# Feed-forward half of a two-layer gated block: values in chunk pairs, rounding on VectorE, four result rows

## The reference

```python
def act_quant(x):
    scale = 127.0 / jnp.clip(jnp.max(jnp.abs(x), axis=-1, keepdims=True), 1e-05)
    return jnp.clip(jnp.round(x * scale), -128, 127) / scale
...
h = bit_linear(x, w1)                              # 512 -> 2048
h = depthwise_conv1d(h.transpose(0, 2, 1), conv_w, conv_b)   # 3 taps along the tokens
h = h.transpose(0, 2, 1)
h = jax.nn.silu(h)
return bit_linear(h, w2)                           # 2048 -> 512
```

## Time and profile before

| | us |
|---|---|
| median of three executions | 2200.01 |
| lowest and highest | 2198.89, 2200.37 |
| profiled execution: time | 2204.66 |
| profiled execution: span of the core | 2202.7 |
| mean granted TensorE clock | 0.938 of full |
| busy in the span: DVE | 1763.1 |
| PE | 1642.2 |
| ACT | 1581.0 |
| POOL | 578.2 |

### The profile page before, as it was taken

The page is one execution under the profiler, slowest core; times in us unless marked ns, Lnnn a source line. Parts: engine busy times, 40 slices in busy tenths (PEclk is TensorE's granted clock), DMA queues, the critical chain, the costliest instruction groups (busy, mean ns, idle before and its releaser), DMA issues.

```text
span 2202.7 us, 24527 instructions
## 1 busy us (share of the span) xinstructions
PE 1642.2 (75%) x9542; PEld 735.0 (33%) x9542; DVE 1763.1 (80%) x2630; ACT 1581.0 (72%) x1157; POOL 578.2 (26%) x438
## 2 busy tenths in 40 slices
PE   7868766886588578659886888899887566667664
...
GB/s 179 1 20 68 20 1 20 67 20 1 1 6 20 44 1 6 6 96 327 199 257 142 68 93 96 96 99 84 80 65 58 24 48 48 48 48 48 39 34 34
DMA packets 104549, 143.65 MB, mean 65 GB/s; under 512 B 8046, under 2 KB 61422, under 8 KB 104050
## 3 DMA queue, kind: packets, MB, share of 16 engines
...
## 4 chain that ended last, share of the span: by engine, by line
ACT 40%; PE 35%; DVE 14%; DMA 5%; issue 3%; POOL 2%; POOLq 0%; SPq 0%; DVEq 0%; ACTq 0%
ACT unit L514 35%; PE psum L1579 5%; PE psum L1613 5%; PE psum L1659 4%; PE psum L1565 4%; DVE hmax_parts L1394 3%; PE psum L1009 3%; PE psum L1015 2%; DMA out_rows<-x3in 2%; DVE unit L423 2%; PE psum L1589 2%; DVE psum L1386 2%; PE psum L1606 1%; DMA xblk<-xnT_scratch 1%; PE psum L1598 1%
## 5 line engine op out<-in xcount | busy, mean ns | idle before, releaser
L514 ACT ACTIVATE unit<-unit 128x4096 f32<-128x4096 f32 x244 | 857.4, 3610 | 0.5 <-DVE unit L423 0.3
L423 DVE TENSOR_SCALAR unit<-feat_proj,text_proj 128x1024 f32<-128x1024 f32 x976 | 667.4, 746 | 66.6 <-PE psum L639 64.7
L639 PE MATMUL psum<-unit,w_pad 128*32 128x512 f32 x3904 | 471.8, 601 | 236.6 <-ACT unit L514 236.6
L639 PEld LDWEIGHTS psum<-unit,w_pad 128*32 128x32 f32 x3904 | 102.2, 109 | 556.9 <-ACT unit L514 399.6
L1659 PE MATMUL psum<-w_q,hidden_q 128*128 128x512 fp8e4 x512 | 144.7, 447 | 77.0 <-ACT hidden_q L1548 39.1
L1637 PE MATMUL psum<-xq_block,w_q 128*128 128x512 bf16 x512 | 140.4, 413 | 45.8 <-ACT hidden L1530 45.4
L1737 POOL TENSOR_TENSOR hidden<-hidden,srow 128x2048 f32<-128x2048 f32 x32 | 144.7, 4524 | 90.4 <-ACT srow L1534 90.4
L680 POOL TENSOR_SCALAR red<-red 128x8 f32<-128x8 f32 x4 | 2.0, 508 | 531.4 <-DVE red L321 531.4
L1518 ACT ACTIVATE psum<-h,conv_b_sb,conv_w_sb 128x512 f32<-128x512 f32 x128 | 98.3, 776 | 47.6 <-DVE h L1380 43.9
L1579 PE MATMUL psum<-xnT_c,wq_sb 128*128 128x256 f32 x512 | 121.7, 392 | 11.0 <-ACT xnT_c L1470 11.0
L547 PE MATMUL psum<-xnT,W_sb 128*128 128x512 f32 x256 | 125.2, 617 | 2.1 <-ACT xnT L465 2.1
...
## 6 DMA issues: line engine op xcount, KB each, us to landing
...
x<-in_x SPq DMA_DIRECT2D x32, 256.0 KB, 2.9
x_scratch<-x SPq DMA_DIRECT2D x32, 256.0 KB, 2.1
x3in<-x_scratch SPq DMA_DIRECT2D x31, 256.0 KB, 2.7
```

The costliest lines, as they stand in the source:

```text
L423: ins = ve.tensor_scalar(units[:, n % 3, k, :], FP[:, bi % 2, k, :], TP[:, k, n:n + 1], None, ALU.add)
L514: ac.activation(units[:, n % 3], units[:, n % 3], ACT.Tanh).then_inc(unit_tanh, 1)
L639: mm = te.matmul(psum[k * TG:(k + 1) * TG, 3 + 2 * grp + half, :], w_pad[:, k, TG - 1 - tt:2 * TG - 1 - tt], units[:, n % 3, k, half * BAN ...
```

## The change

- `H2` and `h2q` are laid out as [8 pairs, tokens, 2]: the values of chunks 2g and 2g + 1 for a token stand side by side. SILU writes every second element; HMAX reduces over pair and chunk-in-pair; HS repeats each value of `srow` twice; W2 loads its weights with a step of two elements.
- HRA and HRB on ACT become HROUND on DVE: one tensor_scalar that adds and subtracts MAGIC and writes bf16. HS of a tile after the first waits until the tile before it is rounded.
- x3in has four buffers, and load_rows(t) waits for the store of tile t - 4.
- `last_tokens` is cut into four parts, issued in the last block ahead of W2 and of OUT of tile i; its SiLU follows SROW. The reload of the four rows is issued among the last tiles. Their matmuls (part 3) stand ahead of the last tile's W2.
- All slots of the feed-forward are new, N2 goes from 437 to 391.

```diff
-    H2 = [sb(f"hidden_{r}", [P, HC, BANK], stack=pd) for r in range(2)]
-    h2q = sb("hidden_q", [P, 2, HC, P], BF16, stack=pd)
-    x3in = sb("x3in", [P, 2, D], stack=pd)
+    H2 = [sb(f"hidden_{r}", [P, HC // 2, BANK, 2], stack=pd) for r in range(2)]
+    h2q = sb("hidden_q", [P, 2, HC // 2, P, 2], BF16, stack=pd)
+    x3in = sb("x3in", [P, 4, D], stack=pd)
...
-    N1, N2, OFF2 = 256, 437, 4330
-    LEN1, LEN2 = 1089, 1113
+    N1, N2, OFF2 = 256, 391, 4330
+    LEN1, LEN2 = 1089, 1028
...
-    W1 = (248, 257, 267, 285, 305, 321, 393, 413, 428, 444, 457, 528, 538, 628, 666, 675)
-    MID = (269, 273, 276, 310, 362, 337, 417, 459, 446, 506, 467, 593, 610, 662, 675, 696)
-    RAW = (267, 303, 331, 426, 456, 547, 655, 689)
-    TAP0 = (283, 291, 308, 322, 369, 377, 431, 477, 504, 552, 574, 637, 649, 675, 683, 709)
-    TAPS = (293, 373, 390, 406, 423, 434, 451, 485, 512, 599, 616, 645, 657, 683, 694, 719)
-    SILU = (314, 386, 403, 421, 437, 450, 499, 526, 611, 632, 644, 660, 670, 696, 715, 735)
-    EDGE = (553, 732)
-    HMAX = (536, 742)
-    HM2 = (805,)
-    HMAXT = (812,)
-    SRED = (822,)
-    S3 = (839,)
-    SROWMM = (845,)
-    SROW = (853,)
-    HS = (859, 906, 953, 993)
-    HRA = (898, 947, 995, 1033)
-    HRB = (920, 968, 1017, 1054)
-    W2 = (937, 985, 1038, 1075)
-    OUT = (967, 1030, 1068, 1105)
+    W1 = (188, 226, 235, 247, 268, 335, 356, 370, 381, 399, 411, 448, 458, 469, 559, 568)
+    MID = (256, 242, 262, 263, 304, 351, 373, 402, 403, 416, 443, 466, 542, 516, 588, 585)
+    RAW = (235, 256, 345, 380, 410, 458, 485, 578)
+    TAP0 = (266, 272, 278, 285, 311, 369, 385, 414, 421, 428, 451, 478, 549, 555, 595, 601)
+    TAPS = (315, 332, 349, 361, 379, 391, 419, 431, 449, 529, 547, 559, 593, 605, 617, 635)
+    SILU = (328, 349, 364, 375, 393, 405, 434, 445, 463, 543, 561, 573, 607, 619, 631, 652)
+    EDGE = (463, 649)
+    HMAX = (477, 659)
+    HM2 = (700,)
+    HMAXT = (707,)
+    SRED = (718,)
+    S3 = (736,)
+    SROWMM = (742,)
+    SROW = (750,)
+    HS = (757, 817, 870, 922)
+    HROUND = (800, 858, 910, 963)
+    W2 = (812, 870, 922, 980)
+    OUT = (852, 904, 973, 1021)
...
-                ve.tensor_reduce(hm[:, k, :], H2[f % 2][:, k * HALF:(k + 1) * HALF, :].rearrange("p c t -> p t c"),
-                                 AX.X, ALU.max, apply_absolute_value=True).then_inc(hmax_step, 1)
+                pairs = slice(k * HALF // 2, (k + 1) * HALF // 2)
+                ve.tensor_reduce(hm[:, k, :], H2[f % 2][:, pairs].rearrange("p g t r -> p t g r"), AX.XY, ALU.max,
+                                 apply_absolute_value=True).then_inc(hmax_step, 1)
...
+            for f, i, t in at2(q, HROUND):
+                V.wait_ge(h_scaled, t + 1)
+                V.wait_ge(w2_mm, t - 1)
...
+                ve.tensor_scalar(h2q[:, t % 2], H2[f % 2][:, :, i * P:(i + 1) * P, :], MAGIC, MAGIC, ALU.add,
+                                 ALU.subtract).then_inc(h2q_done, 1)
             for f, i, t in at2(q, OUT):
+                if f == NF - 1:
+                    last_tokens(i)
                 V.wait_ge(w2_mm, t + 1)
...
-                ac.activation(H2[f % 2][:, c, :], hidden_bank(n), ACT.Silu).then_inc(silu2_done, 1)
+                ac.activation(H2[f % 2][:, c // 2, :, c % 2], hidden_bank(n), ACT.Silu).then_inc(silu2_done, 1)
...
-            for f, i, t in at2(q, HRA):
-                A.wait_ge(h_scaled, t + 1)
-                rows = H2[f % 2][:, :, i * P:(i + 1) * P]
-                ac.activation(rows, rows, ACT.Copy, bias=MAGIC).then_inc(act_step, 1)
-            for f, i, t in at2(q, HRB):
...
+                if f == NF - 1:
+                    A.wait_ge(hmax_step, 3 * NF + 3)
+                    ac.activation(acc4[:, :, :], acc4[:, :, :], ACT.Silu).then_inc(silu2_done, 1)
...
             for f, i, t in at2(q, W2):
+                if f == NF - 1:
+                    last_tokens(i)
                 T.wait_ge(h2q_done, t + 1)
...
-                    mm = te.matmul(psum[:, 4, :], h2q[:, t % 2, c, :], w2_q[:, c, :], start=(c == 0),
+                    mm = te.matmul(psum[:, 4, :], h2q[:, t % 2, c // 2, :, c % 2], w2_q[:, c, :], start=(c == 0),
...
+        def last_tokens(i):
+            if i == 1:
+                T.wait_ge(hmax_step, 3 * NF + 4)
+                T.wait_ge(s_step, 4 * NF)
+                te.transpose(psum[0:NB, 7, 0:P], hm4[:, :], ident[:, :]).then_inc(spread_mm, 1)
+            if i == 2:
+                T.wait_ge(hmax_step, 3 * NF + 7)
+                te.matmul(psum[:, 7, 0:NB], hs4[0:NB, 1:2].broadcast_to([NB, P]), ident[0:NB, 0:NB], start=True,
+                          stop=True).then_inc(spread_mm, 1)
+            if i == 3:
+                T.wait_ge(hmax_step, 3 * NF + 9)
+                for c in range(HC):
+                    mm = te.matmul(psum[0:NB, 7, :], hq4[:, c, :], w2_q[:, c, :], start=(c == 0), stop=(c == HC - 1))
+                mm.then_inc(spread_mm, 1)
...
                 G.wait_ge(bank_read[6], turn[6]["srow", f])
+                if i > 0:
+                    G.wait_ge(h2q_done, t)
                 G.wait_ge(hmax_step, 3 * f + 3)
-                gp.tensor_tensor(H2[f % 2][:, :, cols], H2[f % 2][:, :, cols],
-                                 srow[:, cols].unsqueeze(1).broadcast_to([P, HC, P]), ALU.mult).then_inc(h_scaled, 1)
+                gp.tensor_tensor(H2[f % 2][:, :, cols, :], H2[f % 2][:, :, cols, :],
+                                 srow[:, cols].unsqueeze(1).unsqueeze(3).broadcast_to([P, HC // 2, P, 2]),
+                                 ALU.mult).then_inc(h_scaled, 1)
...
-            S.wait_ge(out_stored[t % 2], 16 * (t // 2))
+            S.wait_ge(out_stored[t % 4], 16 * (t // 4))
```

More of the change, by code:

```diff
@@ L1168, in flamingo @@
     xqb_loaded = sem("xqb_loaded")
-    x3in_loaded = [sem(f"x3in_loaded_{r}") for r in range(2)]
-    out_stored = [sem(f"out_stored_{r}") for r in range(2)]
+    x3in_loaded, TERN_LOADS = tern_loaded, 16 * PARTS
+    out_stored = [sem(f"out_stored_{r}") for r in range(4)]
     spread_mm, w1_mm, mid_ve, mid_gp, tap0_done, tap_step, silu2_done = (
@@ L1276, in flamingo @@
     spread_turn = turns(second("arow", AROWMM), second("srow", SROWMM))
-    act_turn = turns(second("raw", RAW), second("hra", HRA))
     ATT_TURNS = {0: NG, 1: NG, 2: 2 * NG, 4: 2 * NT, 7: 2 * NT}
@@ L1411, in feed_forward @@
                                  ALU.mult).then_inc(s_step, 1)
+            for f, i, t in at2(q, HROUND):
+                V.wait_ge(h_scaled, t + 1)
+                V.wait_ge(w2_mm, t - 1)
+                if t < 2:
+                    V.wait_ge(turn3_mm, NT)
+                    for r in range(GR):
+                        V.wait_ge(x3_stored[r], 16 * TPG * (NG // GR))
+                    for r in range(2):
+                        V.wait_ge(xq_stored[r], 16 * (NG // 2))
+                ve.tensor_scalar(h2q[:, t % 2], H2[f % 2][:, :, i * P:(i + 1) * P, :], MAGIC, MAGIC, ALU.add,
+                                 ALU.subtract).then_inc(h2q_done, 1)
@@ L1412, in feed_forward @@
             for f, i, t in at2(q, OUT):
+                if f == NF - 1:
+                    last_tokens(i)
                 V.wait_ge(w2_mm, t + 1)
                 V.wait_ge(s_step, 4 * f + 4)
-                V.wait_ge(x3in_loaded[t % 2], 16 * (t // 2 + 1) + (16 if t % 2 == 0 else 0))
-                ve.scalar_tensor_tensor(out=x3in[:, t % 2, :], in0=psum[:, 4, :],
-                                        scalar=hs[:, f % 2, 2, i:i + 1], in1=x3in[:, t % 2, :], op0=ALU.mult, op1=ALU.add).then_inc(out_done, 1)
@@ L1453, in vector_C @@
             feed_forward(q)
-        last_tokens()
     def scalar_C():
@@ L1513, in feed_forward @@
                 A.wait_ge(edges_done, edged(f, c))
-                ac.activation(h1[:, c, 2:BANK + 2], hidden_bank(HC * f + c), ACT.Copy).then_inc(act_step, 1)
+                ac.activation(h1[:, c, 2:BANK + 2], hidden_bank(HC * f + c), ACT.Copy).then_inc(raw_copied, 1)
             for f, c, n in at2(q, TAP0):
@@ L1553, in scalar_C @@
             feed_forward(q)
-        A.wait_ge(hmax_step, 3 * NF + 3)
-        ac.activation(acc4[:, :, :], acc4[:, :, :], ACT.Silu).then_inc(silu2_done, 1)
     def tensor_C():
@@ L1786, in load_rows @@
             else:
-                sp.dma_start(x3in[:, t % 2, :], x3_dram[t * P - 1:(t + 1) * P - 1, :]).then_inc(x3in_loaded[t % 2], 16)
+                sp.dma_start(x3in[:, t % 4, :], x3_dram[t * P - 1:(t + 1) * P - 1, :]).then_inc(x3in_loaded[t % 4], 16)
         def store_rows(t):
@@ L1791, in store_rows, with last_rows @@
             skip = 1 if t % TPB == 0 else 0
-            sp.dma_start(out[t * P - 1 + skip:(t + 1) * P - 1, :], x3in[skip:P, t % 2, :]).then_inc(out_stored[t % 2], 16)
+            sp.dma_start(out[t * P - 1 + skip:(t + 1) * P - 1, :], x3in[skip:P, t % 4, :]).then_inc(out_stored[t % 4], 16)
+        ends = slice(SEQ - 1, NTOK, SEQ)
+        def last_rows(i):
+            if i == 0:
+                S.wait_ge(out_stored[0], 16 * NF)
```

(10 more changed lines are left out.)

94 lines of the change are left out of this document (40 added, 54 removed).

## The result

The changed kernel takes 2120.16 us, the median of four executions; the kernel before took 2199.98 beside it (2198.89 to 2200.37). One of the four, the profiled one, ran at a mean granted clock of 0.734 with a span of 2344.3 us; the ratio is worked out from the three others, which lie between 2117.13 and 2122.07. It is 0.9633, with a 95% interval of 0.9614 to 0.9652: 81 us faster, where 66 were forecast. The profile read here is therefore that of a second series of the same kernel: median 2115.06 us (2113.72 to 2117.67), before 2200.44, ratio 0.9616 (0.9601 to 0.963); its profiled execution took 2114.21, span 2112.0.

The account below looks back on a forecast made before the run. The feed-forward stage was taken to run at VectorE's work plus its in-order queue's waits. Seven periods of 50.4 instead of 58.15 us save 54.3, plus start 5.5 and end 6.4: 66 saved, giving 2134 us, range 2118 to 2168.

Parts of the forecast that it names:

- case F: The forecast itself for the whole kernel: a time of 2118 to 2155 us, centred on 2134; chance 0.62.
- A: Rival: HS on POOL is slower with its operand repeated in twos; 2206 us at 1.5 times, 2279 at twice; chance 0.09.
- B: Rival: HMAX on VectorE stays at 7.04 us despite pairs, +42 us, 2176 us; chance 0.06.
- C: Rival: slow HROUND, 2149 us; or strided SILU and W2 loads, 2148; or late TAP0 and SILU, 2163; together 0.16.
- E: Rival: HROUND on VectorE never meets a MID on POOL; period 47.9 us, time 2116; chance 0.04.
- D: Rival: VectorE's waits pile up to the old 11.7 us per block; period 57.4, time 2183 us; chance 0.03.
- HS 4.52 unchanged: HS on POOL was taken to stay at 4.52 us with its second operand repeated in twos.
- the walk's 0.3 + 0.35 + 0.8: Stepping through one block's new slot order, VectorE waits these us for the ends of HS 0, 1 and 2.
- +0.7, the first W2 takes 6.24: Added to the period: a block's first W2 takes 6.24 us, not 3.61, so OUT 0 gets it at 10.5, not 9.8.
- 1.25 twice for MID: In each block, HROUND 0 and HROUND 2 on VectorE each wait 1.25 us for a MID under way on POOL.
- Start, forecast 5.5: Block 0's second HMAX comes 5.5 us sooner, between ends of 2.6 and 7.6, from moved work and shorter HMAX.
- End, forecast 46.5: From the last HMAX to the end takes 46.5 us instead of 52.9, saving 6.4; HROUND 3 ends at 33.5.

Follow-up runs that it names:

- experiment 5: The changed kernel with the rounding back on ACT in two passes and no guard, all else kept: 2181.94 us, ratio 0.9915.
- Experiment 2: The changed kernel with H2 and h2q laid out chunk by chunk as before, all else kept: 2164.4 us.
- experiment 8: The changed kernel with the last tokens' steps behind the last tile on DVE, ACT and PE: 2125.65 us, ratio 0.9659.

## Why the prediction was right, and where its sizes were off

The forecast case F was the one that happened: the stage runs at VectorE's queue, HMAX falls to 4.4 us, HROUND runs in 1.2 us except under a MID. Of the rivals, A (HS slower in twos) had the wrong sign, B and C (HMAX or HROUND slow, W2's loads) fell by the groups above, and the clash that E denied is there. D, waits that pile up again, came true only in experiment 5, with the rounding on ACT. The forecast 2134 lies 14 us above the median and inside its range. It foresaw 66 us, and the medians of the two series differ by 80 and 85; the profiled executions differ by 90.5, some 4 of which lie ahead of the change. The mechanism was right, and the steps below were mis-sized, nearly all of them to the same side.

- **Step "HS 4.52 unchanged", the walk's 0.3 + 0.35 + 0.8.** Failed: HS is 4.076, and in the steady stage VectorE never waits for one. 1.45 us per block, 10 over seven periods. Experiment 2 shows that the layout makes HS shorter.
- **Step "+0.7, the first W2 takes 6.24".** Failed: nothing of it lies on the path. The first W2 of the block takes 3.63 us at 1895.29, and the granted clock is 0.92. 5 us. (By the walk's own numbers the term should have been larger: 4.85 + 6.24 is 11.1, which is 1.3 behind 9.8.)
- **Step "1.25 twice for MID".** Right in kind, too long: in the block shown three roundings meet a MID, not two, and they take 2.09, 2.09 and 1.55 us against 1.22 alone, 2.1 us per block, not 2.5. 3 us over seven periods. So the period is 45.7 of work + 2.1 + 0.2 of waits = 48.0, measured 47.79, forecast 50.4.
- **Start, forecast 5.5, measured 9.88, of which 5.9 to 6.15 are the change's.** About right. From the last LN3 to the second HMAX it is 36.2 us before and 27.3 after: HMAX 2.7, the moved work 4.95, and a TAPS pair of 1.45 that now stands behind the second HMAX and was not counted. But counted from the last L1317, LN3 itself comes 3.0 us later than before, and so I had been right to allow only 5.5 of the 7.6. What delays LN3 was not looked into. This split is worked out from the two timelines, not tried.
- **End, forecast 46.5, measured 44.66.** HROUND 3 ends at 2101.09, 33.75 us after HMAX began, forecast 33.5, but by two errors that cancel: four shorter HS, and a stall nobody had priced. Here is the timeline:

```profile
2082.99 0.22 DVE L1435 TENSOR_TENSOR acc_last<-edges,conv_w_sb 128x64 f32<-128x64 f32 x1
...
2083.13 5.03 PE L1663 MATMUL psum<-w_q,hidden_q 128*128 128x512 fp8e4 x16 [6.08 <-DVE hidden_q L1420]
2083.15 4.11 POOL L1745 TENSOR_TENSOR hidden<-hidden,srow 128x2048 f32<-128x2048 f32 x1 [1.34 <-DVE hidden_q L1420]
2083.37 3.97 DVE L1439 TENSOR_TENSOR acc_last<-acc_last,acc_last_b 128x64 f32<-128x64 f32 x1
...
2090.16 4.06 POOL L1745 TENSOR_TENSOR hidden<-hidden,srow 128x2048 f32<-128x2048 f32 x1 [2.90 <-DVE hidden_q L1420]
...
2101.50 3.62 PE L1679 MATMUL psum<-w_q,hq_last 128*4 128x512 fp8e4 x16 [0.45 <-DVE hq_last L1460]
```

L1439 has 64 elements per partition and ends 0.08 us after the HS that it met; HROUND 1 comes behind it, and HS 2, guarded, waits 2.90. The last tokens' matmuls took 3.62 us and not 5.30, at a granted clock of 1.00 (2101.4 to 2105.2 us); TensorE had been busy for 5.06 of the 5.4 us before them. In experiment 8, where they took 5.30, it had been busy for 3.26 of the 6.8 us before, and the clock over them was 0.68.

**Where the gain comes from.** The parts do not add up. Pairs are worth 28 us in the old order and 49 in the new one; row buffers 5.8 and at most 4; the early last tokens 6 to 10, and the guard about 8, both only at the end. The rounding on VectorE, with the slots made for it, is worth 62 to 66, though VectorE's work per block hardly changes with all edits together (46.4 to 45.7): it takes two ACT passes out of the chain HS, rounding, W2, OUT. VectorE's in-order queue had waited 11.7 us per block in all, most of it with OUT, for W2 and for the reload; now it is 0.2, and 2.1 for the clash. How much of the 62 to 66 is the rounding and how much the slots was not separated: whether slots made for ACT would come near it is open. The 4 us between the two series of the same kernel are unexplained; their intervals overlap.
